# State kept dense: state products in column halves, state times C in row halves, one state addition

## The reference, cut to what matters

```python
lcs = cumsum(dt_c * A)                                   # log decay of each head
M = exp(where(mask, lcs_l - lcs_i, -inf))
G = einsum('blhn,bihn->bhli', C_c, B_c)
intra = einsum('bhli,bihp->blhp', M * G, x_c)
inter = einsum('blh,blhn,bhpn->blhp', exp(lcs), C_c, h)  # state times C
h_new = total_decay * h + einsum('bhl,blhp,blhn->bhpn', M[:, :, -1, :], x_c, B_c)
```

## Time and profile before

| | |
|---|---|
| time, median of 3 runs | 1223.75 us (1223.29 to 1224.1) |
| time of the profiled execution | 1226.72 us |
| its span, first to last instruction | 1224.8 us |
| mean granted TensorE clock | 0.958 |
| busy: PE, DVE, ACT, POOL | 1096.0, 1018.4, 662.8, 653.8 us |

### The profile page before, as it was taken

One profiled execution on the slowest core, in us unless ns is written; L12 is line 12 of the kernel. 1 busy time (PEld: TensorE's weight loads), 2 busy tenths in 40 slices (PEclk: granted clock), 3 DMA queues, 4 the chain that ended last, 5 costly groups with the idle time before them and its releaser, 6 DMA issues.

```text
span 1224.8 us, 28971 instructions
## 1 busy us (share of the span) xinstructions
PE 1096.0 (89%) x8612; PEld 867.0 (71%) x8612; DVE 1018.4 (83%) x2750; ACT 662.8 (54%) x1301; POOL 653.8 (53%) x904
## 2 busy tenths in 40 slices
PE   3899898898898898899889886999999989898996
PEld 2566676575676666666667665888887878787886
DVE  5777977877986986887897778689898989898997
ACT  4776585585676667667667542444343334343442
POOL 7355554564554555555556355246565655555555
PEclk9998998999999999999999887999999999999998
DMA  6000000000000000000000020000000000000000
GB/s 168 3 2 3 2 3 2 1 1 2 1 0 2 1 0 2 1 0 2 1 0 2 3 87 1 1 10 10 11 17 9 9 9 9 9 9 9 9 10 18
DMA packets 15877, 13.53 MB, mean 11 GB/s; under 512 B 2440, under 2 KB 12960, under 8 KB 15776
## 3 DMA queue, kind: packets, MB, share of 16 engines
q1 hardware_dynamic: 15776, 12.49, 3.6%
HBM read 7.77 MB, written 4.19 MB: 10 GB/s over the span
## 4 chain that ended last, share of the span: by engine, by line
PE 37%; DVE 35%; issue 19%; POOL 3%; DVEq 3%; ACT 1%; DMA 1%; SPq 0%; POOLq 0%; ACTq 0%
PE bank L1584 8%; DVE moe_acc L1633 5%; DVE xt L651 4%; PE bank L547 3%; DVE moe_h L1435 3%; PE bank L771 2%; PE bank L549 2%; PE bank L548 2%; PE bank L844 2%; DVE ob L1018 2%; PE bank L1557 2%; PE bank L1558 2%; PE bank L1559 2%; PE bank L827 2%; PE bank L813 2%
## 5 line engine op out<-in xcount | busy, mean ns | idle before, releaser
L1584 PEld LDWEIGHTS bank<-moe_w,moe_hid 128*128 128x128 f32 x2048 | 248.8, 193 | 27.2 <-ACT moe_hid L1568 12.8
L1568 ACT ACTIVATE moe_hid<-bank,moe_b 128x512 f32<-128x512 f32 x256 | 167.6, 688 | 179.8 <-PE bank L1559 179.3
L1584 PE MATMUL bank<-moe_w,moe_hid 128*128 128x128 f32 x2048 | 252.6, 277 | 9.6 <-DVE moe_acc L1633 7.6
L547 PE MATMUL bank<-thi,whi 128*128 128x512 f32 x224 | 120.2, 537 | 57.9 <-DVE cs L691 40.7
L1633 DVE SCALAR_TENSOR_TENSOR moe_acc<-bank,moe_scores,moe_acc 128x128 f32<-128x128 f32 x448 | 126.0, 341 | 33.7 <-PE bank L1584 20.4
L931 POOL TENSOR_TENSOR y<-y,zt 128x256 f32<-128x256 f32 x64 | 46.8, 732 | 140.1 <-DVE y L955 138.3
L1557 PE MATMUL bank<-moe_t_hi,moe_w_hi 128*128 128x512 f32 x256 | 113.9, 445 | 0.0
L1610 POOL TENSOR_TENSOR moe_b_mix<-moe_b_mix 128x512 f32<-128x512 f32 x80 | 106.9, 1337 | 10.2
L856 ACT ACTIVATE m<-bank 128x512 f32<-128x512 f32 x128 | 69.6, 596 | 71.7 <-PE bank L757 71.3
L771 PEld LDWEIGHTS bank<-ct,bt 64*128 64x128 f32 x1024 | 67.6, 188 | 50.1 <-issue 50.1
L1558 PE MATMUL bank<-moe_t_lo,moe_w_hi 128*128 128x512 f32 x256 | 102.6, 401 | 0.0
(11 more groups left out here) (178 smaller groups left out, 2676.4 us busy)
## 6 DMA issues: line engine op xcount, KB each, us to landing
out_dram<-moe_outb SPq DMA_DIRECT2D x16, 256.0 KB, 2.3
moe_w<-in_L_ffn_W_dram SPq DMA_DIRECT2D x1, 1024.0 KB, 5.3
m<-in_L_attn_w_in_proj_dram SPq DMA_DIRECT2D x1, 772.0 KB
xall<-in_L_attn_hidden_dram SPq DMA_DIRECT2D x2, 256.0 KB, 4.5
rows<-parts SPq DMA_DIRECT2D x32, 16.0 KB
moe_b<-in_L_ffn_b_dram SPq DMA_DIRECT2D x1, 512.0 KB, 9.2
mg<-n_L_attn_w_out_proj_dram SPq DMA_DIRECT2D x1, 128.0 KB
dcol<-in_L_attn_D_dram SPq DMA_DIRECT2D x8, 0.1 KB
```

Source lines behind the costliest of these rows:

```text
L547: PE.matmul(bank[:], whi[:, w], thi[:], start=True, stop=False)
L1568: SE.activation(hid[:, e % 2, n, :], up_banks[k % 4][:], ACT.Relu, bias=b1[:, k:k + 1]).then_inc(hid_ready.sem, 1)
L1584: mm = PE.matmul(bank[:, col(i)], hid[:, e % 2, n, col(i)], w2[:, e, n, :], start=n == 0, stop=n == FB - 1, skip_group_check=True)
```

## The change

The state is kept as [128, 4, 32]: pair j has its even head in rows 0 to 63 and its odd head in rows 64 to 127, with no zeros.

- State times C becomes a matmul on the 64 rows of its head, still with 32 stationary columns. `pe_y` now runs four blocks of four heads: state times C of the even heads (rows 0 to 63), intra of the even heads (128 rows), state times C of the odd heads (rows 64 to 127), intra of the odd heads (128 rows). The waits for `mg` stand ahead of each intra block, that for the old state ahead of all.
- The state products become one matmul for each head: 128 rows, 64 stationary columns into column half q, 32 moving columns; 16 instructions for 8.
- `decayed` on POOL and the state addition on DVE work on 128 x 128 elements; DVE has one instruction for two, and so has the memset.

```diff
-    state = keep("state", [P, 2, NP, 2, HD])
-    decayed = keep("decayed", [P, NP, 2, HD])
+    state = keep("state", [P, 2, NP, HD])
+    decayed = keep("decayed", [P, NP, HD])
...
-    state_ready = sig("state_ready", 2)
+    state_ready = sig("state_ready")
...
-        pe.wait_ge(mg_ready.sem, mg_ready.of(t, 1))
-        for slot in range(NH):
-            if slot == HH:
-                pe.wait_ge(mg_ready.sem, mg_ready.of(t, 2))
-            hd = 2 * (slot % HH) + slot // HH
-            q, n = hd % 4, hd // 4
-            PE.matmul(banks[6][q * HD:(q + 1) * HD, col(n)], xtok[:, tp, hd * HD:(hd + 1) * HD], mg[:, tp, slot, :],
-                      start=True, stop=True, skip_group_check=True)
         if due(t - 1):
             pe.wait_ge(state_ready.sem, state_ready.of(t - 1))
-        for hd in range(NH):
-            q, n = hd % 4, hd // 4
-            mm = PE.matmul(banks[6][q * HD:(q + 1) * HD, DI + n * P:DI + (n + 1) * P],
-                           state[:, 1 - tp, hd // 2, hd % 2, :], ct[par][:, hd // 2, col(i)],
-                           start=True, stop=True, skip_group_check=True)
+        apart(pe, t)
+        for odd in range(2):
+            half = slice(odd * NS, (odd + 1) * NS)
+            for j in range(NP):
+                q, n = (2 * j + odd) % 4, j // 2
+                PE.matmul(banks[6][q * HD:(q + 1) * HD, DI + n * P:DI + (n + 1) * P],
+                          state[half, 1 - tp, j, :], ct[par][half, j, col(i)],
+                          start=True, stop=True, skip_group_check=True)
+            pe.wait_ge(mg_ready.sem, mg_ready.of(t, odd + 1))
+            for j in range(NP):
+                hd = 2 * j + odd
+                q, n = hd % 4, j // 2
+                mm = PE.matmul(banks[6][q * HD:(q + 1) * HD, col(n)], xtok[:, tp, hd * HD:(hd + 1) * HD],
+                               mg[:, tp, odd * HH + j, :], start=True, stop=True, skip_group_check=True)
         mm.then_inc(yy_done.sem, 1)
...
-        for j in range(NP):
-            mm = PE.matmul(banks[7][:, col(j, 2 * HD)], btok[:, tp, col(j)], xw[:, tp, col(j, 2 * HD)], start=True,
-                           stop=True,
-                           skip_group_check=True)
+        apart(pe, t)
+        for hd in range(NH):
+            j, q = hd // 2, hd % 2
+            mm = PE.matmul(banks[7][q * NS:(q + 1) * NS, col(j, HD)], btok[:, tp, col(hd, NS)],
+                           xw[:, tp, col(hd, HD)], start=True, stop=True, skip_group_check=True)
         mm.then_inc(ss_done.sem, 1)
...
-        for q in range(2):
-            rows = slice(q * NS, (q + 1) * NS)
-            if last_of_batch:
-                DVE.memset(state[rows, tp, :, q, :], 0.0).then_inc(state_ready.sem, 1)
-                continue
-
-            s = banks[7][rows, 0:DI].rearrange("p (j k d) -> p j k d", k=2, d=HD)[:, :, q, :]
-            DVE.tensor_tensor(state[rows, tp, :, q, :], s, decayed[rows, :, q, :],
+        if last_of_batch:
+            DVE.memset(state[:, tp, :, :], 0.0).then_inc(state_ready.sem, 1)
+        else:
+            DVE.tensor_tensor(state[:, tp, :, :], banks[7][:, 0:P].rearrange("p (j d) -> p j d", d=HD), decayed[:],
                               ALU.add).then_inc(state_ready.sem, 1)
```

More of the change, by code:

```diff
@@ L918, in pool_tile @@
         apart(pl, t)
-        PL.tensor_tensor(decayed[:].rearrange("p j q d -> p j (q d)"),
-                         state[:, 1 - tp, :, :, :].rearrange("p j q d -> p j (q d)"),
-                         tdec[:, tp, :].rearrange("p (j o) -> p j o", o=1).to_broadcast([P, NP, 2 * HD]),
+        PL.tensor_tensor(decayed[:], state[:, 1 - tp, :, :],
+                         tdec[:, tp, :].rearrange("p (j o) -> p j o", o=1).to_broadcast([P, NP, HD]),
                          ALU.mult).then_inc(dec_ready.sem, 1)
```

## The result

The changed kernel took **1260.9 us** in the median of 4 runs (1259.6 to 1265.6), against 1223.9 beside it (1223.3 to 1224.9): ratio 1.0311 with a 95% interval of 1.0287 to 1.0334, so 37 us slower where the prediction said 11 and at most 27. The span of its profiled execution is 1258.3 us, 33.5 more than before, at a mean granted clock of 0.960 (0.958 before). Ratios leave out an execution more than 1.5% above the fastest of its kernel, which is one in the whole document, the slowest of e3_two (1237.0).

A forecast was written before the change was run, and what follows sets the result against it. Neither engine alone was taken to bound the kernel: the chain alternates between DVE parts (dt0 to `cs`) and PE parts. +22.6 us at an unchanged clock, less 11.2 for the clock, gave +11.4: median 1223.75 to 1235 us, range 1216 to 1251.

The forecast's parts named there:

- The turn of the loop: End of a sequence: the chain goes over DVE's y, memset and the turn; no cost was put for PE's turn.
- PE's terms: TensorE, per tile: y products +1.2 us (four blocks of 0.56, 2.24 against 1.03), state products -0.29, together +0.93.
- State products 0.62: TensorE: 16 half-width products with loads side by side, 0.45 plus 0.17 us drain and refill, against 0.91: -0.29 a tile.
- the 1.07 us: TensorE's state products if the column halves' loads came one after another: 16 x 0.056 + 0.17, +0.16 us a tile.
- +2.8 + 1.2 - 0.25 = +3.75: PE parts of a pair of groups: three tiles at 0.93, the last tile's y +1.2, its memset -0.25.
- VectorE: -0.3 us a tile: State addition on DVE: one instruction of 0.285 us for two of 0.60 together; 2 x -0.3 in each DVE part.
- The clock: -11.2 us: PE behind the wait for `cs`: wait shrinks from 2.85 to about 1.6 us; half of up to -22.4 us counted.
- gets it 0.3 earlier: L790 on PE, waiting 5.0 us in 13 for the state, gets it 0.3 us earlier; about as much cost absorbed.
- The overlap of blocks (1207): Rival, TensorE y products: 64- and 128-row blocks overlap, y stays at 1.03 us, total 1207; chance 0.16.
- the serial loads (1245): Rival, TensorE state products: loads come one after another, +9.5 us on the forecast, total 1245; chance 0.08.
- the forecast's sum at an unchanged clock: Whole kernel: +2.55 us a pair times 7 = +17.9, group 0 +2.5, group 15 +2.2; +22.6 us.
- the clock does not recover: Rival, PE's clock: as many stretches at 1.2 GHz as now, 1223.75 + 22.6 = 1246 us; chance 0.24.

The follow-up runs named there:

- e3_two: Changed kernel with two y blocks for four (state times C of all heads, then intra of all): 1229.6 us, ratio 1.0022 to the kernel before.
- e14_shift: Changed kernel, loop body untouched, moved 128 instructions further on by small matmuls ahead of TensorE's loop: 1246.5 us, ratio 1.0187 to the kernel before.
- e21_shift384: Changed kernel, loop body untouched, moved 384 instructions further on by small matmuls ahead of TensorE's loop: 1248.1 us, ratio 1.0206 to the kernel before.
- e4_full: Changed kernel with state products in full-width pairs and two 64-row state additions, as before the change: 1248.1 us, ratio 1.0203 to the kernel before.
- e7_two_full: Changed kernel with two y blocks for four, full-width state products and two state additions: 1221.2 us, ratio 0.9982 to the kernel before.
- e11_pad288: Kernel before with 64 small repeated matmuls (256 more instructions) in TensorE's loop body: 1225.0 us, ratio 1.0015.

## Why the prediction was wrong

**The turn of the loop: no term of the sum (+14 us).** The step that failed first is in the chain: the forecast let it run "over DVE's y and memset and the turn of the loop", took that turn to be as before, and put nothing for PE's. e14_shift and e21_shift384 measure what was left out: 1246.5 and 1248.1 against 1260.9. The clue was in the profile of before: the packets of the program's queue, and the loop body's length, which the change made 144 instructions longer, from 1489 to 1633 (16 matmuls and loads more a tile for the state products, and two empty instructions that carry a wait, by 8 tiles). From the trace of before alone one could have named it as a risk, with the profile page's row of 26 packets as the floor; the price, a wait of some 4 us a turn and 2 to 3 net, needed a run.

**PE's terms: right.** Block 0.56 us and four of them 2.24: measured to the hundredth (306.90 to 309.14 in the kernel after), with the drain of 0.20 us at each switch as "issue":

```profile
346.31 0.36 PEld L835 LDWEIGHTS bank<-mg,xtok 128*32 128x32 f32 x8 [0.20 <-issue]
346.88 0.36 PEld L828 LDWEIGHTS bank<-ct,state 64*32 64x32 f32 x8 [0.20 <-issue]
```

State products 0.62: 0.59, with the loads of column halves side by side, all 16 within 0.55 us in the timeline of the kernel after:

```profile
309.14 0.55 PEld L847 LDWEIGHTS bank<-xw,btok 128*64 128x64 f32 x16 [0.20 <-issue]
```

The Trainium skill, "TensorE: Matmul & The Clock Gate", section Part 3, has a load overlap with matmuls in flight only when its row group differs; the 1.07 us that the forecast made of it did not come. The chain of e14_shift gives the parts of a pair of groups with quick turns, each from the row of `cs`'s release to `dta`:

```profile
336.56 0.71 PE bank L547
...
356.47 0.70 ACT dta L571
...
381.38 0.80 PE bank L547
...
403.55 0.70 ACT dta L571
```

The PE parts take 19.91 and 22.17 us. Before they took 18.11 (331.13 to 349.24, and the earlier trace rows) and 20.43 (374.36 to 394.79, a row of the chain of before that stands below). Together +3.5; forecast +2.8 + 1.2 - 0.25 = +3.75.

```profile
394.79 0.70 ACT dta L571
```

**VectorE: -0.3 us a tile, the second step that failed.** The DVE part between, 356.47 to 381.38, takes 24.91 us, against 25.12 before: -0.2, forecast -0.6. Why is to be seen right behind the addition. Timeline of before, then of after:

```profile
358.78 0.60 DVE L967 TENSOR_TENSOR state<-bank,decayed 64x128 f32<-64x128 f32 x2
359.04 0.72 POOL L931 TENSOR_TENSOR y<-y,zt 128x256 f32<-128x256 f32 x1 [1.38 <-DVE y L955]
359.42 1.08 DVE L647 TENSOR_SCALAR xt<-xraw,cw,cb 128x512 f32<-128x512 f32 x2
```
```profile
423.75 0.28 DVE L964 TENSOR_TENSOR state<-bank,decayed 128x128 f32<-128x128 f32 x1
423.95 1.52 DVE L647 TENSOR_SCALAR xt<-xraw,cw,cb 128x512 f32<-128x512 f32 x2
424.00 0.72 POOL L932 TENSOR_TENSOR y<-y,zt 128x256 f32<-128x256 f32 x1 [1.65 <-DVE y L956]
```

L647 starts 0.44 us sooner after the addition's start (0.20 for 0.64) and takes 0.44 longer (1.52 for 1.08). In both kernels, wherever its first instruction overlaps POOL's product of y and does not begin well ahead of it, it ends 0.28 us after that product ends, to within 0.01 us: in all 15 places before and in 14 of 15 after, whether it begins 0.4 us behind the product or 0.05 ahead. L984 (L987 before) likewise ends 0.08 us after it, in 15 places in each, within 0.02 us, and mostly takes 860 ns for 430. In the one place left over, L647 begins 0.26 us ahead of the product; it then takes its 0.54 us, and POOL's product is the longer one:

```profile
93.43 0.54 DVE L647 TENSOR_SCALAR xt<-xraw,cw,cb 128x512 f32<-128x512 f32 x1
93.69 0.87 POOL L932 TENSOR_TENSOR y<-y,zt 128x256 f32<-128x256 f32 x1
```

So the rows read as DVE's TENSOR_SCALAR waiting until POOL's product is done, and what the addition saves being spent in that wait. The kernels with two additions bear it out: L647 has a mean of 589 ns in e4_full and 581 in e7_two_full, 767 in the changed kernel and in e14_shift. No run moved POOL's product, so the cause is read from the coincidence and not shown by taking it away. The Trainium skill, "SBUF — State Buffer", section Who interferes with whom, has the rule: VectorE and GpSimd share a pair of ports, `tensor_scalar` can take it, and who comes second waits for the whole of the other. The rows agree, except that DVE's record starts 0.05 us ahead of POOL's.

**The clock: -11.2 us, the third.** It rested on a wait for `cs` of 1.6 us. It is 2.1 and 2.2 in turn, mostly since `cs` comes 0.2 earlier and not 0.6. And 1.6 might not have done: e4_full still loses the clock behind 1.87 us. In e14_shift the wait of 336.56 is followed by 3.92 us at a granted clock of 0.56:

```profile
336.55:340.47 3.92, 3.91 (x14) 3.09 (x16) 3.45 (x12) 1.63 (x3) 2.93 (x7) 0.56 0.00 0
```

In the five passes of the loop behind its first turn there are 11 such stretches with 37.5 us, in the kernel before 10 with 34.1: no recovery. Only ahead of the first turn and behind the loop are there fewer (10.3 us for 37.6).

**The other steps.** The state's wait at L790, 5.0 us in 13, is gone, as "gets it 0.3 earlier" had it. GpSimd's `decayed` takes 484 ns (0.2 us less, forecast 0.3), and its wait for ACT stays (7.1 us in 20); it was put at nothing, and nothing on the path speaks against that, but no run has it alone. DVE's wait for y rose from 61.9 us in 33 to 91.2 in 34, 0.9 us each, forecast 1.2. The overlap of blocks (1207) and the serial loads (1245) did not come; 0.20 us for a switch held for 64 to 128 rows and back.

**The sum.** With quick turns the change costs 1246.5 - 1223.9 = 22.6 us, the very figure of the forecast's sum at an unchanged clock. That is partly luck: a pair of groups costs 3.3 us or more, not 2.55 (in the pair above 2 PE parts +3.5 and 2 DVE parts -0.4; from sequence to sequence 92.1 us for 88.8), and the ends less than the +4.7 put there. In the profiled executions, 19.0 us apart by their spans, +1.1 arises ahead of the loop's first turn, +17.8 in the five passes behind it and +0.2 behind the loop; ahead and behind some stretches at 1.2 GHz went. The rival "the clock does not recover", 1246 us at 0.24, had the clock right; with the turn's 14.4 added it makes 1260.

## What to carry to other kernels

Where an engine runs a long loop, count its instructions before and after a change and read the packets of its instruction queue: packets far above what the program's length asks for mean that the body is fetched again in its turns. Moving the loop by half a page of instructions, or writing it out, then gave 13 to 14 us here, more than a third of what the change had lost. Time saved on a VectorE instruction counts only if the next one does not spend it waiting, here by the rows' reading for GpSimd. And price the clock with the waits: a saving that lengthens PE's wait in a thin stretch can cost as much as it gave, while matmuls put into such a wait paid 22 us here.

## What was not expected of the hardware

- A turn of PE's loop has no wait in e14_shift and one of 3.7 to 4.2 us in the changed kernel, by the place of the same body (shifts of 0, 128, 256, 384 instructions: slow, quick, slow, quick).
- A TENSOR_SCALAR of 128x512 on VectorE that takes 533 to 548 ns alone took 1060 beside a TENSOR_TENSOR of GpSimd that began 0.05 us after it, and ended 0.28 us after that.
- What stays open: why only some turns are slow in e3_two (3 of 5) and e11_pad288 (1 of 5), whose bodies did not move between turns, and whether the time that VectorE lost beside GpSimd comes back when GpSimd's product is moved, which no run did.
